# VectorE quantises both slots of g, the b1 splits come later, step as scalar_tensor_tensor, orders of all engines rewritten

## The chip, the cores and the metric

One core of a Trainium2 chip runs the whole kernel. The metric is the device time in microseconds (us) of one execution. The kernel before was timed in three runs; one further execution was recorded by the hardware profiler, and all rows and instants below are of that one.

## The reference

The input x holds 2 x 1024 tokens of 256 numbers. A conditioned adapter comes first, then a feed-forward pair of layers with quantised weights and activations, and x is added again:

```python
# adapter: w_down = down_project * dg + db ; w_up = up_project * ug + ub, from cond_512
y = relu(x @ w_down) @ w_up + x
def bitlinear(x, w, b):            # w1: 1024 x 256, w2: 256 x 1024
    r = x * rsqrt(mean(x * x) + 1e-5)
    scale = 127 / clip(max(abs(r)), 1e-5)
    xq = clip(round(r * scale), -128, 127) / scale
    s = 1 / clip(mean(abs(w)), 1e-5)
    wq = clip(round(w * s), -1, 1) / s
    return xq @ wq.T + b
g = gelu(bitlinear(y, w1, b1), approximate=False)
out = x + bitlinear(g, w2, b2)
```

Each token needs, for y and again for g, its largest absolute value, its mean square and its quantised row. Each weight needs its mean absolute value before it can be quantised.

## The kernel before, in words

The tokens are cut into 8 pairs of two 128-token tiles; a tile is a "slot" (s = 0, 1), a pair is j or k = 0..7. All five engines run an order written out by hand, one list of calls per engine, and meet by semaphores. An engine never looks past an instruction that waits. Line numbers are those of the kernel before.

A pair goes through these steps. TensorE `down` (L262, x times w_down, one call for one or two pairs), ScalarE `relu` (L472), TensorE `up` (L278), VectorE `add_x` (L733, y = up + x), `largest_y` (L653), `first_steps` (L657, the quantisation step from the largest value) and `first_multipliers` (L674, its reciprocal), `quantise_y` (L704, two instructions). TensorE `transpose_q1` (L289), ScalarE `copy_q1t` (L535), TensorE `first_layer` (L308, four matmuls for a slot) and `add_bias` (L315, two matmuls that add b1 out of the rows b1f times the scales invt). ScalarE `gelu` (L511) writes g. VectorE `largest_g` (L648), a step and a multiplier (L657, L674 or L683), then g is quantised: slot 0 on VectorE (`quantise_first`, L689), slot 1 on GpSimd (`quantise_second`, L980). TensorE `transpose_q2` (L332), ScalarE `copy_q2t` (L546), TensorE `second_layer` (L344 and L346), VectorE `combine` (L727), and SyncE stores the pair.

Beside these, ScalarE takes the mean squares, `square_y` (L529) and `square_g` (L519). GpSimd turns them into scales, `dequantisers` (L1001, L1003, L1008), and builds the parts of the inverse scale that carry b1, `inverse_scale` and `inverse_parts` (L1034 to L1056), which TensorE transposes (`transpose_inv`, L297) and ScalarE copies (`copy_invt`, L541). GpSimd also adds b2 to x (`add_b2`, L987, one 128x512 instruction for a pair).

The head of the program prepares the weights. dpk (the condition) is loaded, TensorE multiplies it out (L241, L247), VectorE makes wd (`scale_down`, `shift_down`, L751 and L757) and wu (`scale_up`, `shift_up`, L762 and L769). `split_b1` (L740, two instructions of 41 x 512 elements) turns the loaded rows of b1 into high and low parts; the first `add_bias` needs both. w1 is summed by ScalarE (`abs_sum_w1`, L476) and VectorE (L790), TensorE adds over the partitions (`weight_sum`, L271), VectorE makes the scale iws (L777, L781, L786). Then w1 is rounded (L490 on ScalarE, L800 on VectorE), lowered (L495, L805) and clipped (L809). The same follows for w2 (L476 and L795, L499 and L814, L504 and L818, L822). `keep_busy` (L235) are matmuls of zeros.

SyncE issues the loads in one queue: dpk, upk, x of pair 0 (two halves), w1 (two halves), x of pair 1, w2 (two halves), three loads with two pairs of x each, b2. g has four buffers for a slot, q2 and q2t two. The result of a step of VectorE is used through a semaphore, as here for the quantised g:

```python
def quantise_second(j):            # on GpSimd
    p.wait_ge(m_ready[1], j + 1)
    wait(p, q2t_done[1], j - 1)
    p.tensor_scalar(q2[:, j % 2, 1, :], g[:, j % G_RING, 1, :], m[:, col:col + 1], MAGIC, ALU.mult, ALU.add)
```

Of the kernel before, what the change touches and what calls it, by code (L numbers as in the profile page):

```python
# [4 lines left out]
P = 128  # L5
SLOTS = 2
# [13 lines left out]
def adaln_ffn(nc, x_both, down_pack, up_pack, w1_t, w2_t, b1_rows, b2_rows, out):  # L20
# [3 lines left out]
    with ExitStack() as ctx:  # L24
# [6 lines left out]
        def sem(name):  # L31
            return ctx.enter_context(nc.semaphore(name))
# [48 lines left out]
        neg_half = sb("neg_half", [P, 4])  # L81
        mx = sb("mx", [P, STATS])
# [71 lines left out]
        gsq_done = [sem(f"gsq_done{s}") for s in range(SLOTS)]  # L154
# [76 lines left out]
        def _(pe):  # L231
# [141 lines left out]
            weight_sum(1)  # L373
# [5 lines left out]
            up(2)  # L379
            first_layer(1, 0)  # L380
            transpose_inv(1)
            up(3)
            down(3)
            first_layer(1, 1)
# [3 lines left out]
            up(4)  # L388
            transpose_q2(0, 1)
            transpose_q1(2)  # L390
            sum_w2()
            first_layer(2, 0)
            transpose_inv(2)
            first_layer(2, 1)
            add_bias(2, 0)
            up(5)
            add_bias(2, 1)
            transpose_q2(1, 0)
            second_layer(0, 0)
            transpose_q2(1, 1)  # L400
            transpose_q1(3)
            second_layer(0, 1)
            first_layer(3, 0)
            transpose_inv(3)
            first_layer(3, 1)
            add_bias(3, 0)
            down(4)
            add_bias(3, 1)
            transpose_q2(2, 1)
            transpose_q2(2, 0)  # L410
            second_layer(1, 1)
            transpose_q1(4)
            up(6)
            second_layer(1, 0)
            transpose_inv(4)
            first_layer(4, 0)
            first_layer(4, 1)
            add_bias(4, 0)
            transpose_q2(3, 0)
            second_layer(2, 0)  # L420
            second_layer(2, 1)
            transpose_q1(5)
            add_bias(4, 1)
            up(7)
            transpose_inv(5)
            first_layer(5, 0)
            transpose_q2(3, 1)
            first_layer(5, 1)
            transpose_q2(4, 0)
            add_bias(5, 1)  # L430
            add_bias(5, 0)
            second_layer(3, 0)
            second_layer(3, 1)
            transpose_q1(6)
            transpose_q2(4, 1)
# [5 lines left out]
            second_layer(4, 0)  # L441
            transpose_q1(7)
            first_layer(6, 1)
            transpose_q2(5, 1)
            add_bias(6, 1)
            first_layer(7, 0)
            transpose_inv(7)
            second_layer(5, 0)
# [3 lines left out]
            second_layer(5, 1)  # L452
            transpose_q2(6, 1)
            transpose_q2(6, 0)
            second_layer(6, 1)
            second_layer(6, 0)
            transpose_q2(7, 1)
            transpose_q2(7, 0)
            second_layer(7, 1)
            second_layer(7, 0)  # L460

        @block.scalar
        def _(a):
# [106 lines left out]
            relu(2)  # L570
            copy_q1t(1)
            gelu(0, 1)
            round_w2()
            square_y(2)
            lower_w2()
            copy_invt(1)
            relu(3)
            square_y(3)
            gelu(1, 0)
            copy_q2t(0, 0)  # L580
            gelu(1, 1)
            copy_q1t(2)
            square_g(0, 0)
            copy_q2t(0, 1)
            copy_invt(2)
            square_g(0, 1)
            gelu(2, 0)
            gelu(2, 1)
            copy_q2t(1, 0)
            square_y(4)  # L590
            copy_q1t(3)
            square_g(1, 0)
            copy_q2t(1, 1)
            copy_invt(3)
            square_g(1, 1)
            gelu(3, 0)
            relu(4)
            gelu(3, 1)
            copy_q2t(2, 0)
            square_y(5)  # L600
            copy_q2t(2, 1)
            copy_q1t(4)
            square_g(2, 1)
            copy_invt(4)
            square_g(2, 0)
            square_g(3, 0)
            gelu(4, 0)
            copy_q2t(3, 0)
            square_y(6)
            copy_q1t(5)  # L610
            gelu(4, 1)
            copy_invt(5)
            square_g(3, 1)
            square_g(4, 0)
            copy_q2t(3, 1)
            gelu(5, 1)
            copy_q2t(4, 0)
            gelu(5, 0)
# [4 lines left out]
            square_g(4, 1)  # L623
            square_g(5, 1)
            copy_q2t(5, 0)
            gelu(6, 0)
            copy_q1t(7)
            square_g(5, 0)
            gelu(6, 1)
            copy_invt(7)  # L630
            copy_q2t(5, 1)
            gelu(7, 0)
            square_g(6, 1)
            gelu(7, 1)
            copy_q2t(6, 1)
            copy_q2t(6, 0)
            square_g(6, 0)
            quantise_last()
            square_g(7, 0)
            copy_q2t(7, 1)  # L640
            copy_q2t(7, 0)

        @block.vector
        def _(v):
# [49 lines left out]

            def quantise_last():

                quantise(PAIRS - 1, 1, slice(0, HALF), q2_last[0])
# [15 lines left out]
            def square_last():  # L713
                col = g_col(PAIRS - 1, 1)
                v.wait_ge(last_scaled, 1)
                v.tensor_tensor_reduce(junk[:, (PAIRS - 1) % 2, 1, :], junk_last[:, :], junk_last[:, :], 1.0, 0.0,
                                       ALU.mult, ALU.add, accum_out=ms[:, col:col + 1]).then_inc(gsq_done[1], 1)
# [111 lines left out]
            v.memset(idle[:], 0.0).then_inc(idle_set, 1)  # L829
            v.memset(round_col[:], ROUND)  # L830
# [22 lines left out]
            round_w1(2)  # L853
            clip_w1(0)
            lower_w1(2)
            clip_w1(1)
            clip_w1(2)
            abs_sum_w2()
            add_x(1)
            total_weights(1)  # L860
            largest_y(1)
            weight_scale(1)
            first_steps(-1)
            first_multipliers(-1)
            inverse_weight_scale(1)
            quantise_y(1)
            round_w2()
            largest_g(0, 0)
            add_x(2)
            largest_g(0, 1)  # L870
            largest_y(2)
            second_step(0)
            first_steps(0)
            add_x(3)
            first_multipliers(0)
            second_multiplier(0)
            quantise_first(0)
            lower_w2()
            quantise_y(2)
            clip_w2(0)  # L880
            clip_w2(1)
            largest_y(3)
            add_x(4)
            largest_g(1, 0)
            largest_g(1, 1)
            first_steps(1)
            second_step(1)
            first_multipliers(1)
            second_multiplier(1)
            quantise_first(1)  # L890
            copy_w2_sums()
            largest_y(4)
            quantise_y(3)
            largest_g(2, 1)
            second_step(2)
            add_x(5)
            second_multiplier(2)
            combine(0, 1)
            combine(0, 0)
            largest_g(2, 0)  # L900
            first_steps(2)
            first_multipliers(2)
            quantise_first(2)
            largest_y(5)
            quantise_y(4)
            largest_g(3, 0)
            first_steps(3)
            largest_g(3, 1)
            add_x(6)
            first_multipliers(3)  # L910
            combine(1, 1)
            combine(1, 0)
            second_step(3)
            quantise_first(3)
            second_multiplier(3)
            largest_y(6)
            quantise_y(5)
            largest_g(4, 0)
            combine(2, 0)
            first_steps(4)  # L920
            first_multipliers(4)
            combine(2, 1)
            quantise_first(4)
            add_x(7)
            largest_y(7)
            largest_g(4, 1)
            second_step(4)
# [228 lines left out]
```

## Time and profile before

| | us |
|---|---|
| three runs, median (lowest to highest) | 87.71 (87.54 to 88.22) |
| the profiled execution, own time | 87.23 |
| its span, first to last instruction | 85.5 |
| TensorE busy in the span | 71.1 (83%) |
| VectorE busy | 69.5 (81%) |
| ScalarE busy | 65.2 (76%) |
| GpSimd busy | 50.9 (60%) |

The own time of the profiled execution is 1.7 us more than its span. PE is TensorE, DVE is VectorE, ACT is ScalarE, POOL is GpSimd, SP is SyncE. Instructions of one engine overlap a little: the next starts before the one in front has ended, so a duration in a row is up to 0.1 us more than the distance between two starts.

### The profile page before, as it was taken

The page shows a single profiled execution, that of the slowest core. Times are in us where ns is not written, and L with a number is a line of the kernel's source. Part 1 is how long each engine was busy: PE and PEld are TensorE (multiplying, and loading weights), DVE is VectorE, ACT ScalarE, POOL GpSimd, SP SyncE. Part 2 cuts the span into 40 slices and gives each one's busy share as a digit, 9 for nine tenths or more (in the row PEclk, how much of TensorE's full clock was granted, in tenths as well). Part 3 has the DMA queues.
Part 4 walks back from the last instruction along what each step waited for, and adds up shares of the span by engine and source line. Part 5 has one row for each costly group of instructions (what it writes and reads, how often), then busy time and mean ns, then how long its engine had stood idle before and what let it go on. Part 6 is the DMA issues. An engine that isn't in the chain of part 4 may idle for free.

```text
span 85.5 us, 1679 instructions
## 1 busy us (share of the span) xinstructions
PE 71.1 (83%) x501; PEld 39.7 (46%) x501; DVE 69.5 (81%) x145; ACT 65.2 (76%) x127; POOL 50.9 (60%) x120
## 2 busy tenths in 40 slices
PE   4985765299999799999999979999775999979740
PEld 1522214124443264367356629566542756666630
DVE  2139289983989999999999997999999399799840
ACT  0601481922999899999999999999799698999600
POOL 6800008830579697698998928964887845505900
PEclk9999759858999999999999999999999999999997
DMA  1997999996000000000110003030003021012033
GB/s 20 293 250 286 420 414 437 429 425 280 15 0 0 0 11 0 8 0 0 67 56 8 0 1 122 0 123 8 0 10 113 0 83 39 0 58 76 0 123 123
DMA packets 3212, 9.18 MB, mean 107 GB/s; under 512 B 370, under 2 KB 882, under 8 KB 2820
## 3 DMA queue, kind: packets, MB, share of 16 engines
q1 hardware_dynamic: 3168, 9.05, 28.1%
q8 instruction: 4, 0.07, 0.3%
q10 hardware_dynamic: 36, 0.04, 0.1%
q14 instruction: 4, 0.03, 0.1%
HBM read 6.98 MB, written 2.10 MB: 106 GB/s over the span
## 4 chain that ended last, share of the span: by engine, by line
PE 40%; DVE 27%; issue 9%; ACT 9%; POOL 6%; DMA 4%; ACTq 1%; DVEq 1%; POOLq 0%
PE out_ps L346 8%; PE up_ps L278 8%; PE h L308 7%; DVE mx L648 5%; PE q2t_ps L332 4%; DMA b1f<-b_rows 4%; DVE q L689 4%; DVE y L733 3%; PE h L315 3%; ACT junk L519 3%; DVE xx L727 3%; POOL q L980 3%; PE h L346 2%; DVE step L657 2%; ACT q2t L546 2%
## 5 line engine op out<-in xcount | busy, mean ns | idle before, releaser
L648 DVE TENSOR_REDUCE mx<-g 128x1 f32<-128x1024 f32 x16 | 19.3, 1210 | 1.0 <-ACT g L511 1.0
L511 ACT ACTIVATE g<-h,deq 128x1024 f32<-128x1024 f32 x16 | 17.9, 1121 | 0.4 <-PE h L315 0.3
L519 ACT ACTIVATE junk<-g,sq_scale 128x1024 bf16<-128x1024 f32 x15 | 17.3, 1162 | 0.0
L308 PE MATMUL h<-w1q,q1t 128*128 128x512 f16 x64 | 16.4, 382 | 0.0
L346 PE MATMUL out_ps<-w2q,q2t 128*128 128x256 f16 x112 | 14.4, 273 | 0.0
L278 PE MATMUL up_ps<-wu,act 128*128 128x512 f32 x16 | 10.4, 740 | 2.6 <-ACT act L472 1.7
L980 POOL TENSOR_SCALAR q<-g,m 128x1024 f32<-128x1024 f32 x7 | 9.4, 1340 | 5.0 <-DVE m L683 5.0
L346 PEld LDWEIGHTS out_ps<-w2q,q2t 128*128 128x128 f16 x112 | 11.0, 98 | 1.6 <-issue 0.3
L332 PE MATMUL q2t_ps<-ident,q 128*128 128x128 f16 x128 | 9.6, 220 | 2.3 <-DVE q L689 2.2
L332 PEld LDWEIGHTS q2t_ps<-ident,q 128*128 128x128 f16 x128 | 7.6, 98 | 6.0 <-DVE q L689 4.1
L987 POOL TENSOR_TENSOR xx<-xx,b 128x512 f32<-128x512 f32 x8 | 10.1, 1278 | 0.1
L546 ACT ACTIVATE q2t<-q2t_ps 128x512 f32<-128x512 f32 x16 | 9.5, 607 | 0.8 <-PE q2t_ps L332 0.8
L1003 POOL TENSOR_TENSOR rms<-var,neg_half 128x2 f32<-128x2 f32 (+1 forms) x10 | 9.3, 930 | 0.8
L1001 POOL TENSOR_TENSOR var<-ms,eps_w 128x2 f32<-128x2 f32 (+1 forms) x10 | 3.0, 301 | 11.3 <-ACT junk L519 6.2
L308 PEld LDWEIGHTS h<-w1q,q1t 128*128 128x128 f16 x64 | 5.7, 100 | 6.5 <-issue 1.9
L689 DVE TENSOR_SCALAR q<-g,m 128x1024 f32<-128x1024 f32 (+1 forms) x9 | 7.6, 859 | 0.1
L733 DVE TENSOR_TENSOR y<-up_ps,xx 128x512 f32<-128x512 f32 x8 | 5.5, 684 | 2.7 <-PE up_ps L278 2.7
L727 DVE SCALAR_TENSOR_TENSOR xx<-out_ps,deq,xx 128x256 f32<-128x256 f32 x14 | 6.2, 475 | 1.7 <-PE out_ps L346 1.3
L529 ACT ACTIVATE junk_y<-y,sq_scale 128x256 bf16<-128x256 f32 x14 | 7.1, 519 | 0.3 <-DVE y L733 0.3
L704 DVE TENSOR_SCALAR q<-y,m 128x256 f32<-128x256 f32 x16 | 6.5, 448 | 0.0
L235 PE MATMUL q2t_ps<-idle 128*128 128x512 bf16 x11 | 5.2, 608 | 1.2 <-DVE idle L829 1.2
L657 DVE TENSOR_SCALAR step<-mx 128x1 f32<-128x1 f32 (+2 forms) x18 | 5.8, 326 | 0.4
(109 smaller groups left out, 115.5 us busy)
## 6 DMA issues: line engine op xcount, KB each, us to landing
xx<-x_both SPq DMA_DIRECT2D x3, 1024.0 KB, 13.2
w<-w_t SPq DMA_DIRECT2D x4, 512.0 KB, 8.7
out<-xx SPq DMA_DIRECT2D x7, 256.0 KB, 2.0
xx<-x_both SPq DMA_DIRECT2D x2, 256.0 KB, 4.5
xx<-x_both SPq DMA_DIRECT2D x1, 512.0 KB, 8.7
upk<-up_pack SPq DMA_DIRECT2D x1, 384.0 KB, 3.6
out<-xx SPq DMA_DIRECT2D x2, 128.0 KB, 1.8
dpk<-down_pack SPq DMA_DIRECT2D x1, 129.0 KB, 2.1
```

The costliest lines, as they stand in the source:

```text
L278: pe.matmul(up_flat, act[:, k, :], wu[:, :, :].rearrange("p s n -> p (s n)"), start=True, stop=True)\
L308: pe.matmul(h[s][:, cols], q1t[:, j % 2, s, c, :], w1q[:, c, cols], start=(c == 0), stop=False)
L332: mm = pe.transpose(q2t_ps[s][:, c, :], low_half(q2[:, j % 2, s, P * c:P * (c + 1)]), ident[:, :])
L346: mm = pe.matmul(out_bank(j, s), q2t[:, j % 2, s, c, :], w2q[:, c, :], start=False, stop=(c == FK - 1))
L511: a.activation(g[:, j % G_RING, s, :], h[s][:, :], ACT.Gelu, scale=deq[:, col:col + 1])\
L519: a.activation(junk[:, j % 2, s, :], g[:, j % G_RING, s, :], ACT.Square, scale=sq_scale[:, 0:1], accum_out=ms[:, col:col + 1]).then_inc(gs ...
L546: a.activation(q2t[:, j % 2, s].rearrange("p k t -> p (k t)").bitcast(F32), q2t_words[s], ACT.Copy)\
L648: v.tensor_reduce(mx[:, col:col + 1], g[:, j % G_RING, s, :], AX.X, ALU.max, apply_absolute_value=True)\
L689: v.tensor_scalar(q2[:, j % 2, s, cols], g[:, j % G_RING, s, cols], m[:, col:col + 1], MAGIC, ALU.mult, ALU.add).then_inc(ready, 1)
L980: p.tensor_scalar(q2[:, j % 2, 1, :], g[:, j % G_RING, 1, :], m[:, col:col + 1], MAGIC, ALU.mult, ALU.add).then_inc(q2_ready[1], 1)
L987: p.tensor_tensor(x[:, j], x[:, j], b2[:, :].unsqueeze(1).broadcast_to([P, SLOTS, D]), ALU.add)\
L1003: p.tensor_tensor(rms[:, cols], var[:, cols], neg_half[:, first:last], ALU.pow).then_inc(rms_done, 1)
```

## The change

GpSimd no longer quantises slot 1 of g: `quantise_second` becomes a function of VectorE with the same operands, seven calls. `step_of` becomes a scalar_tensor_tensor whose second factor, 1/127, comes out of a new tile over_q (128 x 4, set once) in place of an immediate. The two `split_b1` calls move: the first from in front of `scale_down` to behind `shift_up`, the second from in front of `scale_up` to behind `add_x(1)`. The last mean square gets a semaphore of its own, gsq_last, for which only the last `dequantisers` waits. The lists of calls of TensorE, ScalarE, VectorE and GpSimd are written in another order. No load, store, tile shape or buffer count changes.

```diff
+        over_q = sb("over_q", [P, 4])
...
             condition_down()
             condition_up()
+            keep_busy(1)
             down(0)
-            keep_busy(1)
+            keep_busy(2)
             up(0)
             keep_busy(3)
             weight_sum(0)
+            down(1)
             transpose_q1(0)
-            down(1)
             up(1)
-            keep_busy(2)
             first_layer(0, 0)
             transpose_inv(0)
-            weight_sum(1)
             first_layer(0, 1)
...
             round_w1()
+            relu(1)
+            lower_w1()
+            abs_sum_w2()
             copy_q1t(0)
-            lower_w1()
-            relu(1)
-            abs_sum_w2()
             copy_invt(0)
...
             def step_of(part, cols):
-                v.tensor_scalar(step[:, cols], mx[:, cols], FLOOR, 1.0 / Q_MAX, ALU.max, ALU.mult)\
-                    .then_inc(step_done[part], 1)
+                v.scalar_tensor_tensor(step[:, cols], mx[:, cols], FLOOR, over_q[:, 0:cols.stop - cols.start],
+                                       ALU.max, ALU.mult).then_inc(step_done[part], 1)
...
+            def quantise_second(j):
+                quantise(j, 1, slice(0, F), q2_ready[1])
...
             set_cond()
-            split_b1(0)
             scale_down()
             shift_down()
-            split_b1(1)
             scale_up()
             shift_up()
+            split_b1(0)
             add_x(0)
...
-                    p.wait_ge(gsq_done[1], i)
+                    p.wait_ge(gsq_done[1], min(i, PAIRS - 1))
+                if i == PAIRS:
+                    p.wait_ge(gsq_last, 1)
```

The end of ScalarE's list changes too. Behind `gelu(7, 1)` stood copy_q2t(6, 1), copy_q2t(6, 0), square_g(6, 0), quantise_last, square_g(7, 0), copy_q2t(7, 1), copy_q2t(7, 0). Now stand there square_g(6, 0), copy_q2t(6, 0), square_g(6, 1), copy_q2t(6, 1), square_g(7, 0), quantise_last, copy_q2t(7, 0), copy_q2t(7, 1).

VectorE at the head of the program before, from the copy that makes cond to the two instructions that make wu:

```order
L745 COPY cond<-dpk 128x256
L740 SCALAR_TENSOR_TENSOR b1f<-b1f,later 41x512
L751 TENSOR_TENSOR wd<-dpk,h 128x256
L757 TENSOR_TENSOR wd<-wd,h 128x256
L740 SCALAR_TENSOR_TENSOR b1f<-b1f,later 41x512
L762 TENSOR_TENSOR wu_gamma<-upk,h 128x256
L769 TENSOR_TENSOR wu<-wu_gamma,h 64x256 x2
```

The same place in the changed program, up to the first add_x (its lines are numbered anew, L744 is split_b1):

```order
L749 COPY cond<-dpk 128x256
L755 TENSOR_TENSOR wd<-dpk,h 128x256
L761 TENSOR_TENSOR wd<-wd,h 128x256
L766 TENSOR_TENSOR wu_gamma<-upk,h 128x256
L773 TENSOR_TENSOR wu<-wu_gamma,h 64x256 x2
L744 SCALAR_TENSOR_TENSOR b1f<-b1f,later 41x512
L737 TENSOR_TENSOR y<-up_ps,xx 128x512
```

Both b1 instructions have left the front of wd and wu.

ScalarE before, from the rounding of its part of w1 (round_w1) to the first gelu; act is the output of relu, q1t and invt are the copies that first_layer and add_bias read:

```order
L490 ACTIVATE w<-w,round_col,iws 128x512
L535 ACTIVATE q1t<-q2t_ps 128x512
L495 ACTIVATE w1q<-w,neg_round 128x512
L472 ACTIVATE act<-h 128x128
L476 ACTIVATE junk_w,asum<-w 128x1024
L541 ACTIVATE invt<-q2t_ps 128x256
L529 ACTIVATE junk_y,ms<-y,sq_scale 128x256 x2
L511 ACTIVATE g<-h,deq 128x1024
```

ScalarE at the same place in the changed program:

```order
L491 ACTIVATE w<-w,round_col,iws 128x512
L473 ACTIVATE act<-h 128x128
L496 ACTIVATE w1q<-w,neg_round 128x512
L477 ACTIVATE junk_w,asum<-w 128x1024
L536 ACTIVATE q1t<-q2t_ps 128x512
L542 ACTIVATE invt<-q2t_ps 128x256
L530 ACTIVATE junk_y,ms<-y,sq_scale 128x256 x2
L512 ACTIVATE g<-h,deq 128x1024
```

relu(1) has moved two places forward, and the copy q1t stands behind the sum over w2.

VectorE in the middle of the changed program, pair 4 and what lies around it (L649 largest_g, L690 a quantised slot of g, L658 a step, L708 quantise_y, L731 combine):

```order
L649 TENSOR_REDUCE mx<-g 128x1
L690 TENSOR_SCALAR q<-g,m 128x1024
L658 SCALAR_TENSOR_TENSOR step<-mx,over_q 128x1
L654 TENSOR_REDUCE mx<-y 128x2
L684 RECIPROCAL m<-step 128x1
L708 TENSOR_SCALAR q<-y,m 128x256 x2
L690 TENSOR_SCALAR q<-g,m 128x1024
L731 SCALAR_TENSOR_TENSOR xx<-out_ps,deq,xx 128x256 x2
```

Two rows L690 stand in a pair, where the program before has one (its L689) and GpSimd had the other.

## Rows read from the trace of the kernel before

**Rows 1.** Busy us by stretch: PE, PEld, DVE, ACT, POOL, then PEclk, DMA share, GB/s.

```profile
30.00:35.00 5.00, 4.82 (x39) 2.72 (x40) 5.00 (x9) 5.00 (x11) 4.47 (x11) 1.00 0.02 7
65.00:70.00 5.00, 3.77 (x38) 2.57 (x37) 3.65 (x6) 4.23 (x8) 3.88 (x10) 1.00 0.00 0
```

**Rows 2.** The same from the first gelu to ScalarE's last copy.

```profile
22.13:80.53 58.40, 53.60 (x430) 31.98 (x431) 54.59 (x104) 56.45 (x106) 42.08 (x87) 1.00 0.08 29
```

**Rows 3.** Timeline of VectorE, head: start, us, line, idle before and releaser.

```profile
5.59 0.74 DVE L740 SCALAR_TENSOR_TENSOR b1f<-b1f,later 41x512 f32<-41x512 bf16 x1 [2.36 <-DMA b1f<-b_rows]
...
12.72 0.67 DVE L790 TENSOR_REDUCE asum<-w 128x1 f32<-128x512 f32 x1
...
14.33 0.17 DVE L786 RECIPROCAL iws<-ws 128x2 f32<-128x2 f32 x1
```

**Rows 4.** Timeline of TensorE, head.

```profile
4.83 1.71 PE L247 MATMUL h<-upk,cond 128*128 128x512 f32 x2 [0.25 <-DMA upk<-up_pack]
7.27 0.66 PE L262 MATMUL h<-xx,wd 128*64 128x128 f32 x8 [0.74 <-DVE wd L757]
...
9.14 1.75 PE L278 MATMUL up_ps<-wu,act 128*128 128x512 f32 x2 [0.89 <-DVE wu L769]
...
14.37 0.66 PE L262 MATMUL h<-xx,wd 128*64 128x128 f32 x8
16.72 2.08 PE L278 MATMUL up_ps<-wu,act 128*128 128x512 f32 x2 [1.69 <-ACT act L472]
...
19.44 1.16 PE L308 MATMUL h<-w1q,q1t 128*128 128x512 f16 x4
```

**Rows 5.** Timeline of ScalarE, head and the first gelu.

```profile
11.06 0.63 ACT L476 ACTIVATE junk_w<-w 128x512 bf16<-128x512 f32 x1
...
14.59 0.81 ACT L490 ACTIVATE w<-w,round_col,iws 128x512 f32<-128x512 f32 x1 [1.97 <-DVE iws L786]
...
16.56 1.05 ACT L476 ACTIVATE junk_w<-w 128x1024 bf16<-128x1024 f32 x1
...
22.13 1.11 ACT L511 ACTIVATE g<-h,deq 128x1024 f32<-128x1024 f32 x1
```

**Rows 6.** DMA issues: x of pair 1, KB, us from issue to landing.

```profile
xx<-x_both SPq DMA_DIRECT2D x1, 512.0 KB, 8.7
```

**Rows 7.** Short stretches of the head, columns as rows 1.

```profile
15.20:16.00 0.80, 0.00 (x0) 0.00 (x0) 0.77 (x3) 0.80 (x3) 0.80 (x3) 1.00 0.98 410
...
17.60:18.40 0.80, 0.80 (x2) 0.15 (x1) 0.80 (x1) 0.10 (x2) 0.23 (x1) 0.50 0.96 399
...
20.00:20.80 0.80, 0.80 (x8) 0.56 (x7) 0.00 (x0) 0.06 (x1) 0.00 (x0) 1.00 0.69 280
```

**Rows 8.** Groups by shape: busy us, mean ns of one, idle before.

```profile
L980 POOL TENSOR_SCALAR q<-g,m 128x1024 f32<-128x1024 f32 x7 | 9.4, 1340 | 5.0 <-DVE m L683 5.0
L689 DVE TENSOR_SCALAR q<-g,m 128x1024 f32<-128x1024 f32 x8 | 7.2, 906 | 0.1
L704 DVE TENSOR_SCALAR q<-y,m 128x256 f32<-128x256 f32 x16 | 6.5, 448 | 0.0
...
L657 DVE TENSOR_SCALAR step<-mx 128x3 f32<-128x3 f32 x6 | 4.1, 676 | 0.3
...
L657 DVE TENSOR_SCALAR step<-mx 128x1 f32<-128x1 f32 x10 | 1.5, 148 | 0.1
```

**Rows 9.** Timeline: a step beside add_b2, and a slot of g quantised with GpSimd quiet.

```profile
46.56 2.50 POOL L987 TENSOR_TENSOR xx<-xx,b 128x512 f32<-128x512 f32 x2
...
46.88 0.98 DVE L657 TENSOR_SCALAR step<-mx 128x3 f32<-128x3 f32 x1
...
50.41 0.74 DVE L689 TENSOR_SCALAR q<-g,m 128x1024 f32<-128x1024 f32 x1
```

**Rows 10.** Timeline of ScalarE, the last gelu and the last two copies.

```profile
74.53 1.10 ACT L511 ACTIVATE g<-h,deq 128x1024 f32<-128x1024 f32 x1
...
79.45 1.08 ACT L546 ACTIVATE q2t<-q2t_ps 128x512 f32<-128x512 f32 x2
```

More of the change, by code:

```diff
@@ L153, in adaln_ffn @@
         ysq_done, ymax_done = sem("ysq_done"), sem("ymax_done")
-        gsq_done = [sem(f"gsq_done{s}") for s in range(SLOTS)]
+        gsq_done, gsq_last = [sem(f"gsq_done{s}") for s in range(SLOTS)], sem("gsq_last")
         gmax_done = [sem(f"gmax_done{s}") for s in range(SLOTS)]
@@ L829, in _ @@
             v.memset(idle[:], 0.0).then_inc(idle_set, 1)
+            v.memset(over_q[:], 1.0 / Q_MAX)
             v.memset(round_col[:], ROUND)
@@ L853, in _ @@
             round_w1(2)
+            clip_w1(1)
+            lower_w1(2)
             clip_w1(0)
-            lower_w1(2)
-            clip_w1(1)
             clip_w1(2)
-            abs_sum_w2()
             add_x(1)
-            total_weights(1)
+            split_b1(1)
             largest_y(1)
-            weight_scale(1)
             first_steps(-1)
             first_multipliers(-1)
-            inverse_weight_scale(1)
             quantise_y(1)
-            round_w2()
+            abs_sum_w2()
             largest_g(0, 0)
             add_x(2)
+            total_weights(1)
+            largest_y(2)
+            first_steps(0)
+            weight_scale(1)
+            first_multipliers(0)
+            inverse_weight_scale(1)
+            quantise_first(0)
+            quantise_y(2)
+            round_w2()
             largest_g(0, 1)
-            largest_y(2)
+            lower_w2()
             second_step(0)
[L873 to L879, printed above, removed]
             clip_w2(0)
             clip_w2(1)
+            second_multiplier(0)
+            add_x(3)
+            quantise_second(0)
             largest_y(3)
+            largest_g(1, 0)
+            first_steps(1)
+            copy_w2_sums()
+            first_multipliers(1)
+            quantise_first(1)
             add_x(4)
-            largest_g(1, 0)
+            quantise_y(3)
             largest_g(1, 1)
-            first_steps(1)
             second_step(1)
-            first_multipliers(1)
             second_multiplier(1)
-            quantise_first(1)
-            copy_w2_sums()
             largest_y(4)
-            quantise_y(3)
+            quantise_second(1)
+            largest_g(2, 0)
+            first_steps(2)
+            combine(0, 0)
+            first_multipliers(2)
+            combine(0, 1)
             largest_g(2, 1)
+            quantise_first(2)
             second_step(2)
@@ L897, in _ @@
             second_multiplier(2)
[L898 to L903, printed above, removed]
+            quantise_y(4)
+            quantise_second(2)
+            combine(1, 0)
+            combine(1, 1)
             largest_y(5)
-            quantise_y(4)
             largest_g(3, 0)
             first_steps(3)
+            first_multipliers(3)
+            add_x(6)
+            quantise_first(3)
             largest_g(3, 1)
[L909 to L912, printed above, removed]
+            combine(2, 1)
             second_step(3)
-            quantise_first(3)
+            combine(2, 0)
             second_multiplier(3)
+            quantise_y(5)
+            quantise_second(3)
             largest_y(6)
-            quantise_y(5)
             largest_g(4, 0)
-            combine(2, 0)
             first_steps(4)
+            add_x(7)
             first_multipliers(4)
-            combine(2, 1)
+            largest_g(4, 1)
             quantise_first(4)
-            add_x(7)
+            second_step(4)
             largest_y(7)
-            largest_g(4, 1)
-            second_step(4)
             second_multiplier(4)
             quantise_y(6)
-            largest_g(5, 1)
+            quantise_second(4)
             combine(3, 1)
@@ L933, in _ @@
             largest_g(5, 0)
+            first_steps(5)
+            largest_g(5, 1)
+            first_multipliers(5)
             second_step(5)
-            first_steps(5)
+            quantise_first(5)
             second_multiplier(5)
-            first_multipliers(5)
-            quantise_first(5)
+            quantise_second(5)
             quantise_y(7)
@@ L1084, in _ @@
             inverse_parts(1)
+            add_b2(0)
+            dequantisers(0)
             weight_constants(1)
-            add_b2(0)
             add_b2(1)
-            quantise_second(0)
-            dequantisers(0)
             inverse_scale(2)
@@ L1092, in _ @@
             add_b2(2)
-            quantise_second(1)
+            add_b2(3)
             dequantisers(1)
@@ L1096, in _ @@
             inverse_parts(3)
-            add_b2(3)
-            quantise_second(2)
             dequantisers(2)
@@ L1117, in _ @@
             inverse_parts(7)
+            add_b2(5)
             dequantisers(6)
-            quantise_second(6)
+            add_b2(6)
+            add_b2(7)
             dequantisers(7)
```

162 lines of the change are left out of this document (76 added, 86 removed).

## The prediction

> **What bounds the kernel now.** I read the windows of busy time first. From 30 us on TensorE, VectorE and ScalarE are all full: 4.8, 5.0 and 5.0 of 5 us in 30 to 35, with GpSimd at 4.5 [rows 1]. Between 65 and 70 they drop to 3.8, 3.7 and 4.2, so late in the program the engines wait for each other. In the middle nothing can be won by making one engine faster alone.
>
> ScalarE has least to spare. From its first gelu at 22.13 [rows 5] to the end of its last copies at 79.45 + 1.08 = 80.53 [rows 10] lie 58.4 us, of which it is busy 56.45, VectorE 54.59 and TensorE 53.60 [rows 2]: idle 1.9, 3.8 and 4.8 us. What follows is fixed: last second_layer, combine and store, 85.5 - 80.53 = 5.0 us. So the time is three terms: when ScalarE starts its first gelu, what it then waits, and the 5.0 us.
>
> The head, 22.1 us, is the loose part. In the timelines VectorE waits 2.36 us for the rows of b1 to land, then spends 0.74 us on them, and only then makes wd [rows 3]. TensorE waits 0.74 us for wd, 0.89 for wu and 1.69 for the relu of pair 1 [rows 4]. ScalarE waits 1.97 us for the weight scale iws [rows 5].
>
> **The change, part by part: the head.** I follow it step by step with the durations of the rows.
>
> 1. b1 splits. With the first behind shift_up, wd no longer waits for the b1 rows. down(0) then stands behind condition_up, which ends at 4.83 + 1.71 = 6.54, and one keep_busy: about 6.8 for 7.27. The second split no longer stands between wd and wu, so up(0) starts near 8.1 for 9.14 [rows 4]: 1.0 us. The first split now fills the time in which VectorE waits for up(0); the second, 0.74 us [rows 3], is done before the first add_bias reaches TensorE. Both cost nothing while TensorE is behind; without that cover the price is 0.7 us.
>
> 2. iws. VectorE's sum over its part of w1 (0.67 us) starts at 12.72 [rows 3]. It can't start before w1 has landed; ScalarE takes its own part at 11.06 [rows 5]. With y one us earlier it starts near 11.3, 1.4 us sooner. ScalarE's last sum ends at 11.8 in both kernels, so it allows this. iws comes at 14.5 - 1.5 = 13.0.
>
> 3. relu(1) in front of lower_w1. x of pair 1 lands 8.7 us after its issue at 3.6, so at 12.3 [rows 6]; down(1), before at 14.37 [rows 4], goes right then. round_w1 takes 13.0 to 13.8 (0.81 [rows 5], starts overlap), relu(1) 0.2 more, and up(1) starts at 14.0 for 16.72: 2.7 us.
>
> 4. First layer. It waits for q1t, which now stands behind lower_w1 and the sum over w2: 14.0 + 0.6 + 1.1 (1.05 [rows 5]) + 0.5 = 16.2. VectorE has clipped w1 by 15.9 (its seven instructions behind iws, 3.0 us as before). Two keep_busy matmuls (0.85 us at the low clock) are gone from before it. So first_layer(0, 0) starts at 16.2 for 19.44 to 19.65 [rows 4]. Behind it nothing new is long: two slots of 0.9, the inverse parts (ready about 16.9) and the bias. First gelu: 22.13 - 3.5 = 18.6.
>
> TensorE's clock carries risk here. It was idle at 15.2 to 16.0, and from 16.3 the granted clock was 0.50, that is 1.2 of 2.4 GHz, until 19.5 under a busy TensorE; then it was 1.00 again [rows 7]. So up(1) took 2.08 us. I count 2.1 us for it after the change too, hence no loss.
>
> **The middle.** VectorE gains seven quantisations, 0.74 us each with GpSimd quiet [rows 9]: +5.2 us. It loses stalls. While GpSimd works on a long instruction, a tensor_scalar of VectorE takes as long as the rest of that instruction: the step at 46.88 takes 0.98 us and ends at 47.86, where the first of two add_b2, of 1.28 us, ends [rows 9]. The three-column steps take 0.676 us in the mean and the one-column steps 0.148; quantised slots take 0.906 against 0.74 [rows 8]. Removable at most: 6 x 0.53 = 3.2, 8 x 0.17 = 1.3. An instruction of quantise_y takes 0.448 in the mean for a quarter of the elements of a slot of g; the smallest instructions cost 0.148 [rows 8], so by size it should take 0.148 + (0.74 - 0.148) / 4 = 0.30, and 16 x 0.15 = 2.4. That is 6.9 in all. GpSimd's quantising was 9.4 us [rows 8] of 19.4 us of long instructions; the eight add_b2 of 1.25 [rows 9] stay. I take half, 3.4 us. VectorE's net is +1.8 us, 56.4 in place of 54.6: as full as ScalarE.
>
> The new form of the step is not in the trace on such small tiles. From below it is 0.148 us, as the one-column steps [rows 8]; from above 0.74, as b1 with 512 columns [rows 3]. The instruction nearest in size and kind is the one-column reciprocal or step, so I take 0.17 us, 18 x 0.02 = 0.4 us, which stands in the allowance below. A gain below the old form is excluded by the second tensor it reads. At 0.74 the 18 would cost 10 us more; 0.3 is the most I keep for the range, 2.7 us.
>
> The Trainium skill speaks against this edit. Its page "SBUF — State Buffer", section "Who interferes with whom", says that a Vector instruction with two SBUF inputs also contends with a GpSimd instruction that reads SBUF, and both mx and over_q lie in SBUF. The trace has no such pair of instructions, so no row decides. By it the steps would still stall on add_b2; what that costs by rows is rival C.
>
> GpSimd loses 9.4 us, and its 5.0 us of waits for VectorE's multipliers [rows 8]. It was not the bound, but dequantisers and inverse_parts were queued behind quantise_second. They now come early. A wait is added too: the last dequantisers for gsq_last, with only deq and the last combines behind it; nothing else queues there.
>
> **The end.** The list behind gelu(7, 1) has one mean square more (1.13 us), 6.0 us for 5.0 before (74.53 + 1.0 to 80.53). It is the same work in another place, so it adds nothing to the 56.5.
>
> **The sum.** Measured to the end of ScalarE's last copy, 80.53 before. ScalarE's side: 18.6 + 56.45 = 75.1 without any wait, 77.0 with its old 1.9. VectorE's side: 18.6 + 56.4 = 75.0, and 78.8 with its old idle time of 3.8. So the gain lies between 1.7 (VectorE keeps all its idle time) and 5.4 (nobody waits). I walked through the new lists with the durations above, pair by pair; there ScalarE stays some 3 us ahead of before up to pair 4, and its last copy ends at 76, gain 4.6. Such a walk knows no delay that isn't in a row, and the new steps are 0.4 of it, so I take 0.9 off: gain 3.7 us. 87.23 - 3.7 = 83.5 for the profiled execution. The median of the runs is 0.5 higher; 87.71 - 3.7 = **84.0 us**.
>
> **Rivals.**
>
> A. The head's gain is given back in the middle: VectorE, now the fullest engine, keeps its idle time. Then the gain is the lower end, 1.7: 87.7 - 1.7 = 86.0. For it: VectorE at 5.0 of 5 [rows 1]. Against: its waits were on TensorE and gelu, which come earlier too.
>
> B. The clock. TensorE is idle before up(1) and again stays at 0.50, now through the first layers: two slots at 1.7 for 0.9 us and the bias, up to 1.7 us on the first gelu. 84.0 + 1.7 = 85.7. For it: the fall at 16.3 after a quiet stretch [rows 7]. Against: up(1) alone is 2.1 us of busy time before the first layer.
>
> C. The steps still stall on GpSimd. At most four of the steps meet an add_b2 as at 46.88, 0.98 - 0.15 = 0.83 us each: 84.0 + 3.3 = 87.3 at the most, and 1 us if one or two do: 85.0.
>
> D, the other side. VectorE is the sole bound and nothing of its idle time refills. It gets 5.2 us for quantising and saves only a third of the stalls, 2.2 us, while the head's 3.5 us are lost because add_x and largest_g of pairs 1 to 3 stand behind more work. 87.7 + 5.2 - 2.2 = 90.7 if all is lost; half of the head's gain kept, 89.0. It decides once stalls saved plus head gain are below 5.2. For it: three full engines. Against: 3.8 us of idle time behind the first gelu [rows 2].
>
> **How the numbers follow.** Forecast 0.48, A 0.17, B 0.12, C 0.15, D 0.08. The range reaches from 82.4 (the walk's gain with a shorter wait, 5.3) to 86.4, past A, B and the lower end of C. A measurement tells about 1% of this kernel from no change, 0.9 us: below 86.8 is faster. D and the upper end of C lie beyond: faster 0.88, same 0.06, slower 0.06.
>
> **What would show it.** First gelu at 18 to 19.5 us; up(1) near 14; iws near 13. No wait of more than 0.8 us on VectorE between 30 and 60. ScalarE full, 4.8 of 5 or more, up to 65. Steps of 0.15 to 0.2 us, and if some take near 1 us beside add_b2, C is right. Granted clock 1.00 from 16.5. The prediction is wrong if the first gelu stays behind 20.5, or if VectorE's last square ends after 78.5.

## The result and the profile after

The changed kernel takes 84.3 us (83.47 to 84.93, four runs), the kernel before 87.62 in the same comparison: ratio 0.958, 95% interval 0.948 to 0.968. Forecast were 84.0 us and a range of 82.4 to 86.4. A later comparison gave 84.1 us, ratio 0.960 (0.951 to 0.969). A median is over all executions, while a ratio leaves out those more than 1.5% above the fastest of their kernel, and the first profiled execution of the changed kernel is one of these.

| profiled execution | before | after | after, second profile |
|---|---|---|---|
| own time / span, us | 87.23 / 85.5 | 84.93 / 83.2 | 84.12 / 82.4 |
| first gelu starts | 22.13 | 20.70 | 19.73 |
| from there to ScalarE's last copy | 58.4 | 58.1 | 58.2 |
| from the last copy to the end | 5.0 | 4.4 | 4.5 |

The second profile is from that later comparison. The first is 0.6 us above the median of its kernel. Its span fell by 2.3 us: 1.4 in the head, 0.3 in the middle, 0.6 at the end. In the second it fell by 3.1: 2.4, 0.2 and 0.5. The lines below are of the first.

TensorE's timeline in the head of the changed kernel, the same places as in [rows 4]:

```profile
4.79 2.07 PE L248 MATMUL h<-upk,cond 128*128 128x512 f32 x2 [0.21 <-DMA upk<-up_pack]
...
8.35 1.10 PE L279 MATMUL up_ps<-wu,act 128*128 128x512 f32 x2
...
12.09 0.35 PE L272 MATMUL out_ps<-asum,ones 128*128 128x3 f32 x2 [2.00 <-DVE asum L794]
12.37 0.66 PE L263 MATMUL h<-xx,wd 128*64 128x128 f32 x8
...
14.17 2.07 PE L279 MATMUL up_ps<-wu,act 128*128 128x512 f32 x2 [0.81 <-ACT act L473]
16.31 1.89 PE L309 MATMUL h<-w1q,q1t 128*128 128x512 f16 x4
```

The waits for wd and wu are gone, up(1) starts at 14.17 for 16.72, the first layer at 16.31 for 19.44. But its four matmuls take 1.89 us for 1.16 before. The window says why (columns as rows 1), and ScalarE's timeline shows the first gelu waiting for it:

```profile
15.00:20.00 5.00, 4.94 (x12) 1.23 (x10) 4.58 (x12) 2.62 (x8) 2.48 (x11) 0.50 1.01 418
20.70:78.76 58.06, 53.73 (x436) 33.17 (x437) 54.95 (x112) 56.63 (x106) 34.59 (x79) 1.00 0.09 31
```

```profile
20.70 1.12 ACT L512 ACTIVATE g<-h,deq 128x1024 f32<-128x1024 f32 x1 [0.89 <-PE h L316]
...
78.16 0.60 ACT L547 ACTIVATE q2t<-q2t_ps 128x512 f32<-128x512 f32 x1 [0.43 <-PE q2t_ps L333]
```

The granted clock was 0.50 from 15 to 20 us. The second window answers to [rows 2]: VectorE is busy 54.95 us for 54.59, though it has seven quantised slots more; GpSimd 34.6 for 42.1. Over the whole span VectorE is busy 70.3 us for 69.5. The groups show where the room came from, beside [rows 8]:

```profile
L690 DVE TENSOR_SCALAR q<-g,m 128x1024 f32<-128x1024 f32 x15 | 11.6, 778 | 0.1
L708 DVE TENSOR_SCALAR q<-y,m 128x256 f32<-128x256 f32 x16 | 4.8, 341 | 0.0
L658 DVE SCALAR_TENSOR_TENSOR step<-mx,over_q 128x1 f32<-128x1 f32 x10 | 2.3, 226 | 0.2
L658 DVE SCALAR_TENSOR_TENSOR step<-mx,over_q 128x3 f32<-128x3 f32 x6 | 1.5, 255 | 0.6
```

In the mean a quantised slot takes 778 ns for 906, an instruction of quantise_y 341 for 448, a three-column step 255 for 676. The one-column steps alone grew, 226 for 148. VectorE's and GpSimd's timelines show where:

```profile
33.74 0.72 DVE L658 SCALAR_TENSOR_TENSOR step<-mx,over_q 128x3 f32<-128x3 f32 x1
...
67.69 0.64 DVE L658 SCALAR_TENSOR_TENSOR step<-mx,over_q 128x1 f32<-128x1 f32 x1
```

```profile
31.94 2.50 POOL L992 TENSOR_TENSOR xx<-xx,b 128x512 f32<-128x512 f32 x2
...
67.03 1.28 POOL L992 TENSOR_TENSOR xx<-xx,b 128x512 f32<-128x512 f32 x1
```

Both steps end where an add_b2 ends (34.46 and 34.44; 68.33 and 68.31). A third step, 0.41 us with one column, ends in the same way. So the new form still waits for GpSimd. By the rule of the Trainium skill that the prediction named ("SBUF — State Buffer", "Who interferes with whom": two SBUF inputs contend with a GpSimd instruction that reads SBUF), the trace agrees.

### The profile page after: what moved, and what is told of

Read it like the earlier page. It is cut to its first block, busy times and chain, and to the rows that moved or that the text cites. A ratio compares the mean times of both kernels' runs of the same rounds, so it can differ in the third digit from the quotient of the medians.

```text
span 83.2 us, 1680 instructions
## 1 busy us (share of the span) xinstructions
PE 71.4 (86%) x501; PEld 40.3 (48%) x501; DVE 70.3 (84%) x153; ACT 65.3 (79%) x127; POOL 44.5 (54%) x113
## 4 chain that ended last, share of the span: by engine, by line
ACT 34%; PE 22%; DVE 18%; issue 13%; DMA 4%; POOL 3%; DVEq 1%; POOLq 1%; SPq 0%; ACTq 0%
ACT g L512 9%; ACT junk L520 9%; PE h L309 6%; DVE mx L649 4%; DMA upk<-up_pack 4%; DVE q L690 4%; ACT junk_y L530 4%; PE up_ps L279 3%; PE h L248 2%; POOL rms L1010 2%; ACT q2t L547 2%; ACT q1t L536 2%; PE out_ps L347 2%; PE q2t_ps L333 2%; DVE mx L654 2%
## 5 line engine op out<-in xcount | busy, mean ns | idle before, releaser
L649 DVE TENSOR_REDUCE mx<-g 128x1 f32<-128x1024 f32 x16 | 19.3, 1209 | 1.8 <-ACT g L512 1.6
L512 ACT ACTIVATE g<-h,deq 128x1024 f32<-128x1024 f32 x16 | 18.2, 1142 | 1.2 <-PE h L316 1.2
L309 PE MATMUL h<-w1q,q1t 128*128 128x512 f16 x64 | 17.7, 411 | 0.6 <-ACT q1t L536 0.5
L1008 POOL TENSOR_TENSOR var<-ms,eps_w 128x2 f32<-128x2 f32 (+1 forms) x10 | 2.3, 233 | 21.5 <-ACT junk_y L530 12.9
L690 DVE TENSOR_SCALAR q<-g,m 128x1024 f32<-128x1024 f32 (+1 forms) x16 | 12.1, 760 | 0.1
L1010 POOL TENSOR_TENSOR rms<-var,neg_half 128x2 f32<-128x2 f32 (+1 forms) x10 | 10.2, 1019 | 0.8
L279 PE MATMUL up_ps<-wu,act 128*128 128x512 f32 x16 | 9.6, 687 | 0.9 <-ACT act L473 0.8
L731 DVE SCALAR_TENSOR_TENSOR xx<-out_ps,deq,xx 128x256 f32<-128x256 f32 x14 | 6.3, 472 | 0.2 <-issue 0.2
L316 PE MATMUL h<-b1f,invt 9*128 9x512 bf16 x32 | 6.4, 406 | 0.0
L654 DVE TENSOR_REDUCE mx<-y 128x2 f32<-128x512 f32 x8 | 5.4, 675 | 0.0
L236 PE MATMUL q2t_ps<-idle 128*128 128x512 bf16 x11 | 4.2, 504 | 1.2 <-DVE idle L833 1.2
L542 ACT ACTIVATE invt<-q2t_ps 128x256 bf16<-128x256 bf16 x8 | 3.3, 412 | 2.2 <-PE q2t_ps L298 2.2
```

Source lines behind the costliest of these rows:

```text
L279: pe.matmul(up_flat, act[:, k, :], wu[:, :, :].rearrange("p s n -> p (s n)"), start=True, stop=True)\
L309: pe.matmul(h[s][:, cols], q1t[:, j % 2, s, c, :], w1q[:, c, cols], start=(c == 0), stop=False)
L512: a.activation(g[:, j % G_RING, s, :], h[s][:, :], ACT.Gelu, scale=deq[:, col:col + 1])\
L649: v.tensor_reduce(mx[:, col:col + 1], g[:, j % G_RING, s, :], AX.X, ALU.max, apply_absolute_value=True)\
L690: v.tensor_scalar(q2[:, j % 2, s, cols], g[:, j % G_RING, s, cols], m[:, col:col + 1], MAGIC, ALU.mult, ALU.add).then_inc(ready, 1)
L1010: p.tensor_tensor(rms[:, cols], var[:, cols], neg_half[:, first:last], ALU.pow).then_inc(rms_done, 1)
```

## The experiments

Each experiment has one profile, and where an instant or a stretch is given it is of that one. Theory 1: the head sets the gain, and what lies behind it runs its 62 to 63 us from the first gelu to the end whatever comes first. Theory 2: the gain is made behind the head. Where two kernels have different heads I compare by that stretch, "gelu to end": 63.4 us before, 62.5 after.

**The changed kernel again.**

> The changed kernel once more, beside the three below. Theory 1 (the head sets the gain): ratio to the kernel before 0.955 to 0.965, first gelu between 18.6 and 20.7 us, earlier where the granted clock of TensorE is 1.00 in 15 to 20 us and later where it is 0.50. Theory 2 (the middle sets it): the time does not follow the first gelu.

84.1 us. In this profile the granted clock was 1.00 throughout, first gelu 19.73, gelu to end 62.7. iws came later than in the first profile (13.85 for 12.88), and first_layer with it (17.28 for 16.31), so a full clock alone did not bring 18.6.

**Head and rest apart.** One kernel has the new lists up to the second gelu in the kernel before, the other the old lists up to there in the changed one. This is where ScalarE's list of the first one turns from new to old, against the changed kernel:

```diff
             relu(2)
             gelu(0, 1)
             copy_q1t(1)
-            square_y(2)
             round_w2()
-            copy_invt(1)
+            square_y(2)
             lower_w2()
+            copy_invt(1)
...
```

> The kernel before with the new lists up to the second gelu of pair 0 alone: b1 splits later, relu(1) forward, keep_busy moved; slot 1 of g stays on GpSimd, the step stays tensor_scalar. Theory 1: the first gelu comes at 18.6 to 20.7 us as in the changed kernel, and the middle keeps most of it: 85.3 to 86.2 us against 87.6. Theory 2 (the gain is that of the freed GpSimd and the new order behind the head): the middle gives it back, 87.2 to 88.

> The changed kernel with the old lists up to the second gelu of pair 0, so with the old head and all that is new behind it. Theory 1: first gelu at 22.1 us as before, ScalarE's stretch from there to its last copy 57.5 to 58.4 us for 58.4, time 86.0 to 87.0. Theory 2: 84.5 to 85.3.

Head alone: 86.65 us, ratio 0.984 (0.966 to 1.001); first gelu 19.95, gelu to end 64.9. Rest alone: 87.03 us, ratio 0.991 (0.986 to 0.997); first gelu 22.49, gelu to end 62.5. Neither theory as I put it: alone the two bring 1.6% and 0.9%, the first with an interval that reaches 1.00, and together 4%. The head alone starts its first gelu 2.2 us earlier than before and then takes 1.5 us longer to the end (64.9 for 63.4). The new middle keeps its length (62.5 to 62.8 from starts at 18.8 to 22.5). ScalarE in the head alone shows where the 1.5 us go, L498 being round_w2, L528 square_y and L510 the first gelu of pair 1:

```profile
23.88 1.24 ACT L498 ACTIVATE w<-w,round_col,iws 128x1024 f32<-128x1024 f32 x1 [0.72 <-DVE iws L783]
...
28.30 0.51 ACT L528 ACTIVATE junk_y<-y,sq_scale 128x256 bf16<-128x256 f32 x1 [0.61 <-DVE y L730]
...
29.30 1.09 ACT L510 ACTIVATE g<-h,deq 128x1024 f32<-128x1024 f32 x1
```

From the first gelu to that of pair 1 it takes 9.35 us (29.30 - 19.95), where the kernel before takes 7.89 (30.02 - 22.13). From there to the end both take 55.5 us, so behind pair 1's first gelu nothing is lost. In front of it ScalarE now waits 0.72 us for the scale of w2, which comes at 23.68 for 21.98 before, because the new lists of the head take the sum over w2 later. The changed kernel has square_y(2) in front of round_w2, as the cut above shows, and waits there 0.36 us in its second profile and not at all in its first. That this place is what the head needs is an argument; it was not tried by itself. VectorE stalls in the head alone as in [rows 8]:

```profile
L686 DVE TENSOR_SCALAR q<-g,m 128x1024 f32<-128x1024 f32 x8 | 7.3, 907 | 0.1
L654 DVE TENSOR_SCALAR step<-mx 128x3 f32<-128x3 f32 x6 | 4.3, 716 | 0.3
```

A quantised slot takes 907 ns for 906 before, a three-column step 716 for 676.

**The b1 splits alone.**

```diff
             set_cond()
-            split_b1(0)
             scale_down()
             shift_down()
-            split_b1(1)
             scale_up()
             shift_up()
+            split_b1(0)
...
             add_x(1)
+            split_b1(1)
```

> The kernel before with the two b1 splits moved as in the change and nothing else. Theory 1: wd, wu and iws come 0.5, 1.0 and 1.4 us earlier (up(0) near 8.1 us, iws ready at 13.1), and since iws heads the chain w1 rounded, relu(1), up(1), first layer, the first gelu comes 1.0 to 1.4 us earlier, at 20.7 to 21.1 us; time 86.2 to 87.0 beside 87.6 to 88.4. Rival: the chain from relu(1) has slack or the granted clock takes it back; first gelu at 22 us, no change.

86.66 us, ratio 0.987 (0.979 to 0.994). First gelu 20.46, gelu to end 63.3. Two moved instructions give 1.3%, a third of the whole change. Of the 1.67 us part is another start of the loads: ScalarE's first sum, which waits for w1, began at 9.25 for 9.80. The profiled execution, 85.55 us, is the fastest of the five. With relu(1) in its old place up(1) already starts at 14.53 for 16.72. From iws to the first layer it takes 4.94 us (12.31 to 17.25) as before (14.50 to 19.44), and 3.26 in the changed kernel: this 1.7 us is what the new order behind iws is worth, with two keep_busy fewer in front of the first layer.

**The step as tensor_scalar again.**

```diff
-                v.scalar_tensor_tensor(step[:, cols], mx[:, cols], FLOOR, over_q[:, 0:cols.stop - cols.start],
-                                       ALU.max, ALU.mult).then_inc(step_done[part], 1)
+                v.tensor_scalar(step[:, cols], mx[:, cols], FLOOR, 1.0 / Q_MAX, ALU.max, ALU.mult)\
+                    .then_inc(step_done[part], 1)
```

> The changed kernel with the step as tensor_scalar again. Theory 1 (both forms wait while GpSimd works on add_b2, as the three steps of 0.72, 0.64 and 0.41 us in the changed kernel do): the same, within 0.3 us from the first gelu to the end, and steps of up to 0.7 us at the same three places. Rival (scalar_tensor_tensor escapes GpSimd in part): more and longer stalled steps than in the changed kernel, 0.5 to 1.5 us slower.

83.53 us, ratio 0.951 (0.944 to 0.957), with the changed kernel at 0.958 and 0.960: not slower. First gelu 18.20, the earliest of all, with iws at 12.03; gelu to end 63.1, 0.3 to 0.6 us longer than with the new form, which one profile can't tell from noise. The groups and two places of its timeline:

```profile
L658 DVE TENSOR_SCALAR step<-mx 128x3 f32<-128x3 f32 x6 | 2.5, 410 | 0.6
L658 DVE TENSOR_SCALAR step<-mx 128x1 f32<-128x1 f32 x10 | 1.5, 149 | 0.2
```

```profile
22.38 1.05 DVE L658 TENSOR_SCALAR step<-mx 128x3 f32<-128x3 f32 x1
...
65.73 0.15 DVE L658 TENSOR_SCALAR step<-mx 128x1 f32<-128x1 f32 x1
```

```profile
22.13 1.27 POOL L992 TENSOR_TENSOR xx<-xx,b 128x512 f32<-128x512 f32 x1 [0.93 <-DMA b<-b_rows]
...
65.08 1.27 POOL L992 TENSOR_TENSOR xx<-xx,b 128x512 f32<-128x512 f32 x1
```

The steps take 4.0 us in all for 3.8 in the changed kernel. I expected stalls at the same three places. Of these only the three-column step stalls, 0.73 us, and another three-column step at 22.38 takes 1.05 us, up to the end of an add_b2 that it did not meet in the first profile of the changed kernel. The two one-column steps in the midst of an add_b2 (65.73 and 70.83) take 0.15 us each, where the new form took 0.64 and 0.41.

**No b2.** b2 is left out of x; a memset of one column gives the signal. So GpSimd has no addition of 128x512 left; its longest in the middle are the powers of 128x4 in `dequantisers`, 1.0 to 1.25 us.

```diff
-                p.tensor_tensor(x[:, j], x[:, j], b2[:, :].unsqueeze(1).broadcast_to([P, SLOTS, D]), ALU.add)\
+                p.memset(tick[:, j:j + 1], 0.0)\
```

> The changed kernel without the addition of b2 (left out: b2 is not added to x; a memset of one column signals in its place), so that GpSimd has no long instruction left. Theory 1: no step over 0.2 us and no quantised slot over 0.8; VectorE gets 1.3 us of steps and 0.5 to 1 us of quantisation back, and from the first gelu to the end it is 0.5 to 1.5 us shorter than 62.5. Rival (ScalarE alone sets the pace): the stalls go and the time stays, under 0.3 us.

83.41 us, ratio 0.949 (0.942 to 0.956). Gelu to end 61.8 for 62.5 to 62.8: what add_b2 costs, stalls of VectorE and GpSimd's own time together, is 0.7 to 1.0 us in this one profile. In the median the kernel is 0.1 us below step_old in the same comparison, which is no difference. No step is long any more:

```profile
L659 DVE SCALAR_TENSOR_TENSOR step<-mx,over_q 128x1 f32<-128x1 f32 x10 | 1.6, 158 | 0.2
L659 DVE SCALAR_TENSOR_TENSOR step<-mx,over_q 128x3 f32<-128x3 f32 x6 | 1.0, 163 | 0.6
```

That is also the price of the new form alone: 0.16 us, for 0.17 assumed. A quantised slot takes 752 ns. One that runs beside a power (46.81 beside 46.34 to 47.59) takes 0.74 us, so not every long instruction of GpSimd holds VectorE up.

**Slot 1 of g on GpSimd again**, in GpSimd's old list, and then put into its new list.

```diff
             quantise_first(0)
...
-            quantise_second(0)
...
         @block.gpsimd
...
             inverse_parts(2)
+            quantise_second(0)
             add_b2(2)
```

> The changed kernel with slot 1 of g quantised on GpSimd again, in GpSimd's old list; everything else new. Theory 1 (the seven quantisations cost VectorE what the stalls beside GpSimd's cost it): from the first gelu to the end 63.0 to 64.0 us for 62.5, so 0.5 to 1.5 us slower, with VectorE's quantised slots at 0.9 us again and its steps longer. Rival (VectorE is the bound and the move only loads it): 61.5 us or less, 1 us faster.

> The changed kernel with slot 1 of g quantised on GpSimd again, this time put into GpSimd's new list where its multiplier is ready by the trace of the changed kernel, so that combine doesn't wait for add_b2 of GpSimd's old list. Theory 1: of the 5.4 us that the old list cost from the first gelu to the end the waits of combine for GpSimd (9.1 us) go, and 0.5 to 2 us remain over the changed kernel's 62.6. Rival: quantising on GpSimd is itself what costs, 3 us or more remain. Second rival: VectorE is the bound and the seven quantisations are better off GpSimd's side, 62 us or less.

Old list: 89.06 us in the median of ten executions between 87.76 and 91.39, ratio 1.007 (1.001 to 1.012); the profiled one took 89.33, gelu to end 67.9. By the ratios that is 4 to 5% or some 4 us above the changed kernel, where I expected 0.5 to 1.5. The waits of VectorE name the cause, combine queued for add_b2 and the scales:

```profile
DVE xx L728 <- POOL deq L1011: 5.8, 3, 2.6
DVE xx L728 <- POOL xx L988: 3.3, 1, 3.3
```

Fitted list: 85.02 us, ratio 0.970 (0.963 to 0.976), gelu to end 63.7. So the move to VectorE is worth 1.0 us in the new order, beside the one fitted list that was tried, though VectorE is busy 4.4 us less without it (65.9 for 70.3). It waits where it didn't: 3.0 us for the scales, for 0.7, and 3.0 for gelu, for 1.6. The groups of the fitted kernel say something else too:

```profile
L690 DVE TENSOR_SCALAR q<-g,m 128x1024 f32<-128x1024 f32 x8 | 6.7, 843 | 0.0
L705 DVE TENSOR_SCALAR q<-y,m 128x256 f32<-128x256 f32 x16 | 4.8, 343 | 0.0
L658 DVE SCALAR_TENSOR_TENSOR step<-mx,over_q 128x3 f32<-128x3 f32 x6 | 2.1, 343 | 0.6
```

GpSimd quantises its seven slots here, and still quantise_y takes 343 ns for 448 in the kernel before and the three-column step 343 for 676. These two gains, 3.7 us of busy time together, came with the new order and not with the move.

**TensorE's clock.** Ten keep_busy more where TensorE was idle, or all but the first five away:

```diff
             keep_busy(3)
+            keep_busy(7)
             weight_sum(0)
             down(1)
             transpose_q1(0)
+            keep_busy(3)
             up(1)
```

> The changed kernel with seven more keep_busy matmuls in front of weight_sum(0) and three in front of up(1), where TensorE stood idle for 2.0 and 0.8 us. Theory 1: the granted clock stays 1.00 through the first layers, up(1) takes 1.1 us for 2.07 and each slot of the first layer 0.9 for 1.7; first_layer still starts at 16.3 (it waits for the copy of q1t), the first gelu comes at 18.7 us for 20.7, and the time is 1 to 2 us under the changed kernel's. Rival: VectorE or the middle takes it back, under 0.4 us of gain; or the keep_busy come at the low clock and delay weight_sum, slower by 0.5 us or more.

> The kernel with ten more keep_busy matmuls once more, on the chip of the three below. Clock 1.00 through the head again, first gelu 18.2 to 19 us, 62.8 us from there to the end, 83.1 to 83.8 us.

> The changed kernel without any keep_busy but the first five (six fewer matmuls of zeros). Theory 1: the granted clock is 0.50 in the head, at the latest from up(1) on; first gelu at 20.7 to 21.5 us, and 1.0 to 2.5 us slower than the kernel with ten more. Rival (keep_busy does nothing for the clock): the same time within 0.3 us.

With ten more: 83.47 us, ratio 0.953 (0.941 to 0.966), beside 84.1 for the changed kernel in the same comparison, so 0.6 us where I expected 1 to 2; the second time 83.24, ratio 0.948 (0.944 to 0.953). Without: 84.09, ratio 0.958 (0.953 to 0.963), like the changed kernel. I expected 1.0 to 2.5 us between the two and found 0.85. The windows of the warm kernel and of the one without:

```profile
15.00:20.00 5.00, 3.91 (x26) 1.55 (x26) 4.80 (x12) 3.50 (x10) 3.19 (x11) 1.00 1.00 416
```

```profile
10.00:15.00 5.00, 2.79 (x15) 2.06 (x16) 4.51 (x13) 4.31 (x12) 1.98 (x4) 0.56 1.04 430
15.00:20.00 5.00, 4.94 (x22) 1.50 (x20) 4.57 (x13) 3.33 (x9) 2.93 (x12) 0.76 1.00 419
```

Without them the clock fell at 10.6 us and was back at 17.4, where in the first profile of the changed kernel it fell at 13.7 and was back at 20.5; the first gelu came at 19.37. The missing matmuls need not be the cause: with them in place it fell at 11.3 to 11.4 and was back at 18.2 to 18.3 in two other profiles of this head (gpsimd_back and no_b2). Warm, the first gelu came at 18.83 and 19.82, the second time behind an iws at 13.94.

The mean granted clock of each execution is on record. With ten more it was 0.99 to 1.00 in all twelve. In the ten of the changed kernel it was 1.00 in three and 0.96 to 0.98 in seven. So the ten matmuls keep the clock, and the kernel with them is 0.6 to 0.9 us faster. That the clock is the whole of this is not shown: the three executions of the changed kernel at 1.00 took 84.08 to 84.18 us. One of them is the second profile, with iws at 13.85; the warm one with iws at 13.94 took 84.11, the same. By its median the warm kernel is the fastest of the complete kernels.

**The copy of q1t in front of the sum over w2**, on the warm kernel.

> The same, with the copy of q1t of pair 0 on ScalarE in front of the sum over w2 instead of behind it. First layer waited 1.0 us for that copy. Theory 1: it now starts when w1 is clipped, 0.3 to 0.5 us earlier, and the first gelu with it; a quarter or more of that is given back in the middle, so 0.1 to 0.4 us faster than the kernel above. Rival: the sum over w2 comes later and holds round_w2, no gain or a loss.

83.5 us, ratio 0.952 (0.948 to 0.956), no gain over 83.24. The first layer starts at 15.75 for 16.12, but then TensorE waits for the inverse parts of GpSimd:

```profile
15.75 1.02 PE L309 MATMUL h<-w1q,q1t 128*128 128x512 f16 x4 [0.68 <-DVE w1q L812]
17.23 0.28 PE L298 MATMUL q2t_ps<-identb,inv 128*128 128x128 bf16 x2 [0.46 <-POOL inv L1062]
```

The next link of the head lies on GpSimd, right behind the old one; the first gelu came at 18.82, for 18.83 and 19.82 without the edit. So my theory of 0.1 to 0.4 us failed, and its rival of no gain held, though by this wait and not by the sum over w2.

## Why the prediction was right, point by point

The forecast of 84.0 us was right for 84.3 and 84.1 measured. In its terms the head was too large and the end too small, and that these made up for each other is luck.

- b1 splits, step 1: up(0) at 8.35 for 8.1 forecast. Right.
- iws, step 2: 12.88 + 0.17 = 13.05 for 13.0. Right.
- relu(1), step 3: up(1) at 14.17 for 14.0, and 2.07 us long as counted. Right.
- First layer, step 4: start 16.31 for 16.2. Right. These instants move from one execution to the next. In the second profile all came about 1 us later; over six profiles of this head (both of the changed kernel, step_old, no_b2, gpsimd_back, gpsimd_fit) the first layer started at 15.46 to 17.28, 16.3 in the mean.
- The first gelu was forecast at 18.6 and came at 20.70. Here a term failed, "two slots of 0.9 us": at the clock of 0.50 they took 1.9 each. From the start of the first layer to the first gelu it took 4.39 us there, 2.45 in the second profile at full clock and 2.5 to 4.4 over the six, for 2.4 counted. This was rival B, with 1.7 us at most; it was 2.1. The first gelu of the six came at 18.2 to 20.7, 19.5 in the mean, so the head gave 2.6 us in the mean of these profiles and not 3.5.
- Both marks of a wrong forecast were crossed in the first profile: the first gelu at 20.70 for 20.5, and VectorE's last square, which ended at 77.36 + 1.22 = 78.58 for 78.5. The clock was not 1.00 from 16.5 but from 20.5. In the second profile neither was crossed: 19.73, and 76.53 + 1.22 = 77.75.
- The middle, 58.4 to 58.2 forecast, 58.06 and 58.20 measured. The length was right by two terms that were each off. VectorE's net was put at +1.8 us and was +0.4 in this window and +0.8 over the span, because the stalls saved were 4.4 us or more and not 3.4. And they were saved mostly by the new order, not by GpSimd's quantising less, as the fitted list shows. The room was not turned into fewer waits of ScalarE, whose work is 56.6 of these 58.1 us.
- The end, forecast unchanged, gave 0.6 us. TensorE's last matmul ends 1.3 us behind ScalarE's last copy for 1.7, since second_layer(7, 0) runs while the last transposes are copied. Of this only 0.1 us arrives: the last two combines now wait 0.71 us for the scales, and end 2.2 us behind the copy for 2.3. The rest is the stores. SyncE stores slot 0 first. Before, combine(7, 0) came last, so both stores were issued behind it, from 82.89 on; now it comes first, and the first store is issued at 80.60, 0.36 us in front of the end of the last combine.
- Rival C came true in kind (a three- and a one-column step, 0.72 and 0.64 us, and a one-column step of 0.41). It is 0.7 to 1.0 us by the run without b2, together with the slots of g that wait there and GpSimd's own time. Rivals A and D fell: the new middle keeps its length from any start.
- The allowance of 0.9 us "for what isn't in a row" was meant for the walk through the middle. That the head came later than forecast by as much, 19.5 for 18.6 in the mean, is luck too.
- The prediction said that no row decides about the step's new form, as the trace before had no instruction of VectorE with two SBUF inputs beside one of GpSimd. There was one pair, with the waiting on GpSimd's side:

```profile
78.89 1.22 DVE L716 CUSTOM_DVE_ANT_0 junk<-junk_last 128x1024 bf16<-128x1024 f32 x1
```

```profile
79.09 1.07 POOL L1008 TENSOR_TENSOR deq<-step,rms 128x2 f32<-128x2 f32 x1
```

L716 multiplies junk_last by itself. The multiplication of 128x2 on GpSimd took 1.07 us, up to 80.16 where L716 ends at 80.11, and 0.20 us at 81.31 with L716 gone. So a row spoke for rival C.

## What to carry to other kernels

Follow the head of a program instruction by instruction: a small operation that waits for a late load, in front of the ones on the path, cost 1.3% here, and the order behind the weight scale another 1.7 us up to the first layer. Forecast a head for both levels of the clock: here the same two slots took 1.9 us and 3.8. A piece of work can be worth moving onto the fuller engine: seven quantisations raised VectorE's busy time by 4.4 us beside the fitted list and still gained 1.0 us, because what waited for GpSimd no longer did. Test that by moving the work back into lists that fit it, or the order gets mixed up with the move. And an order belongs to all its lists: with one old list among the new ones the kernel was some 4 us slower.

## What the runs showed that was not expected

- A one-column tensor_scalar doesn't wait for GpSimd's add_b2 (0.149 us in the mean, 0.15 in the midst of one, twice), a three-column one does (up to 1.05). The scalar_tensor_tensor with both inputs in SBUF waits with one column too (0.64). The new form saved 0.2 us of busy time in all and nothing of the median: already in the old form the three-column steps fell from 676 to 410 ns. The old form on the warm kernel, both gains together, was not tried.
- Six keep_busy matmuls taken away cost nothing; ten more gained 0.6 to 0.9 us. The same kernel ran its head with the clock at 1.00 in one profile and at 0.50 in another.
- Head and rest gave 1.6% and 0.9% alone and 4% together. The difference of 1.5% is not clear of the intervals. The profile of the head alone has a cause for it: 1.5 us lost in front of pair 1's first gelu.
